# A four-layer graph network on one core: one run of activations ahead of the block norm, transfers issued in another order between stages, and maxima taken block by block

## What is computed

```python
# layer 0: two mean convolutions around a small MLP
h = relu(mean_in(x) @ Wl.T + bl + x @ Wr.T); h = relu(h @ M1.T + b1) @ M2.T + b2
out = mean_in(h) @ Wl2.T + bl2 + h @ Wr2.T
# layer 1: messages over the edges, then over the nodes; mlp = silu(batchnorm(. @ W + b))
msg = mlp(concat([x[src], edge_attr])); agg = mean of msg over dst
out = mlp(concat([x, agg]))
# layer 2: out = segment_sum((x @ W + b)[src] * att, dst)
# layer 3: three hops h = segment_sum(norm * h[src], dst), then h @ W + b
```

## Time and profile before

| | |
|---|---|
| median of 3 runs | 7751.79 us (7751.47 to 7754.62) |
| profiled execution, its own time | 7756.2 us |
| span of the profiled execution | 7754.3 us |
| busy PE, PEld, DVE, ACT, POOL | 5193.7, 4676.6, 2918.5, 1301.6, 3566.4 us |
| mean granted clock of PE | 0.823 of full speed |

### The profile page before, as it was taken

The page is one execution under the profiler, slowest core; times in us unless marked ns, Lnnn a source line. Parts: engine busy times, 40 slices in busy tenths (PEclk is TensorE's granted clock), DMA queues, the critical chain, the costliest instruction groups (busy, mean ns, idle before and its releaser), DMA issues.

```text
span 7754.3 us, 162987 instructions
## 1 busy us (share of the span) xinstructions
PE 5193.7 (67%) x62971; PEld 4676.6 (60%) x62971; DVE 2918.5 (38%) x5181; ACT 1301.6 (17%) x1613; POOL 3566.4 (46%) x3543
## 2 busy tenths in 40 slices
PE   5999989994444444444466336656656656999999
PEld 5999959993222222222255236655555656999999
DVE  6999931112111111111178434444444444111111
ACT  3777730000000000000066300000000000000000
POOL 2111100005777777777765177777777773000000
PEclk9999989996666666666699567777777778999999
DMA  4444408883333333333376113434434434898887
GB/s 118 186 180 184 185 34 263 275 277 101 94 94 95 95 95 95 95 95 95 92 232 194 36 34 104 110 94 110 111 94 111 111 94 139 274 293 281 275 273 242
DMA packets 559744, 1154.73 MB, mean 149 GB/s; under 512 B 155246, under 2 KB 367216, under 8 KB 546464
## 3 DMA queue, kind: packets, MB, share of 16 engines
q1 hardware_dynamic: 234784, 794.54, 32.1%
q10 hardware_dynamic: 215616, 239.17, 9.4%
q0 software_dynamic: 108896, 114.33, 7.3%
HBM read 898.83 MB, written 248.88 MB: 148 GB/s over the span
## 4 chain that ended last, share of the span: by engine, by line
POOL 36%; PE 26%; issue 16%; DVE 2%; ACT 2%; DMA 2%; DVEq 1%; POOLq 0%; ACTq 0%; SPq 0%; PEldq 0%
POOL gath L366 36%; PE banks L863 21%; PE banks L967 2%; DMA gath<-tab_l,idx 1%; DVE area L1898 1%; ACT gath L1387 1%; ACT banks L1384 1%; PE banks L544 1%; PE banks L556 1%; PE banks L1547 1%; PE banks L957 1%; DVEq L1910 0%; DMA gath<-counts 0%; ACT feat L1349 0%; PE banks L1542 0%
## 5 line engine op out<-in xcount | busy, mean ns | idle before, releaser
L366 POOL DMA_INDIRECT gath<-tab_l,idx x3328 | 3149.1, 946 | 2109.7 <-DMA idx<-src_idx 1096.3
L1556 PE MATMUL banks<-area,ones 128*128 128x448 f32 (+1 forms) x1040 | 674.0, 821 | 1205.1 <-DVE area L1840 1205.0
L967 PE MATMUL banks<-oneh,gath 128*64 128x128 f32 x3328 | 697.9, 404 | 891.9 <-DMA gath<-tab_l,idx 891.9
L1556 PEld LDWEIGHTS banks<-area,ones 128*128 128x128 f32 x1040 | 308.6, 312 | 1528.4 <-issue 1527.5
L967 PEld LDWEIGHTS banks<-oneh,gath 128*64 128x64 f32 x3328 | 658.5, 219 | 917.5 <-DMA gath<-tab_l,idx 917.5
L1840 DVE TENSOR_TENSOR area<-gath,banks 128x448 f32<-128x448 f32 (+1 forms) x256 | 138.9, 584 | 1660.1 <-DMA gath<-tab_l,idx 1653.6
L829 ACT CAST wide<-banks 128x784 uint16<-128x784 f32 x784 | 651.4, 858 | 221.9 <-PE banks L786 221.6
L798 PE MATMUL banks<-feat,wide 128*128 128x129 f16 x9604 | 670.7, 220 | 0.3 <-ACT wide L829 0.3
L798 PEld LDWEIGHTS banks<-feat,wide 128*128 128x128 fp8e4 x9604 | 606.3, 97 | 0.6 <-issue 0.5
L863 PE MATMUL banks<-wide,gath 128*128 128x128 f16 x9604 | 557.4, 220 | 20.4 <-DMA gath<-counts 20.4
L863 PEld LDWEIGHTS banks<-wide,gath 128*128 128x128 fp8e4 x9604 | 544.8, 98 | 22.2 <-issue 21.8
(11 more groups left out here) (257 smaller groups left out, 6542.4 us busy)
## 6 DMA issues: line engine op xcount, KB each, us to landing
gath<-counts SPq DMA_DIRECT2D x294, 784.0 KB, 4.5
oneh<-counts SPq DMA_DIRECT2D x294, 784.0 KB, 4.5
counts<-wide SPq DMA_DIRECT2D x98, 1568.0 KB, 5.2
gath<-counts ACTq DMA_DIRECT2D x98, 784.0 KB, 4.7
area<-counts ACTq DMA_DIRECT2D x98, 784.0 KB, 4.8
area<-edge_feat SPq DMA_DIRECT2D x128, 448.0 KB, 4.3
gath<-tab_l,idx POOLq DMA_INDIRECT x3328, 2.4
edge_h<-area ACTq DMA_DIRECT2D x128, 416.0 KB, 5.1
```

The source lines that it names most:

```text
L366: pool.indirect_dma_start(out=to[:, h, c, 0:H], out_offset=None, in_=table[:, :], in_offset=bass.IndirectOffsetOnAxis(ap=idx[:, slot, c:c ...
L967: last = T.matmul(window[h][0:H, :], near[:, h, c, :], oneh[:, h, c, :], start=(c == 0), stop=(c == C - 1))
L1556: ins = T.matmul(bank[n][:, 0:(hi - lo) * H], ones[:, :], src[:, lo:hi, :].rearrange("p c f -> p (c f)"), start=first and lo == 0, stop=la ...
```

## The change

1. **Setup.** ACT, no longer SP, issues the write of `fine_heads`, as its first instruction. DVE takes the maximum of each block as soon as that block is copied, `fine_dve` runs after the sixth block, and the last reduction is over 14 numbers. The bias fold of the residual is gone from here; `keep_root` adds the bias. The low parts of `x` are written by DVE in the first slot of the count matrix, behind its first one-hots, and PE waits for them at its first sums.
2. **MLP to dense pass.** `keep_root` takes the block's maximum too. High and low parts of `y` are written in seven pieces of 14 tiles, and PE waits piece by piece. SP begins to load the counts when the products of the count matrix are done.
3. **Dense to edge pass.** The first four lists are loaded ahead of the last table stores. ACT issues the load of `rdeg`, when the first edge group has been added; DVE waits for it only ahead of `z_means`.
4. **Norm stage.** ACT activates all 14 blocks in a row; then the turns have nine steps. PE has four pairs of banks and writes block b when block b - 4 has left them. `row_scale` moves to POOL, as step 9. The first four lists and the attention weights are issued behind the last store, ahead of the wait for it.

The core of the diff:

```diff
...
+x_peak = y_low = sem("block_maxima_then_y_low_pieces")
...
-d_norm = Turns("d_norm", 11, of=d_l1)
+d_norm = Turns("d_norm", 9, of=d_l1)
+s_silu, s_rows = p_conv2.onehot, p_conv2.summed
...
-def load_lists(sp, n_win, used, edge=False):
-    with sp.Fori(0, n_win) as w:
-        with sp.Fori(0, ITERS // 2) as j:
-            for v in range(2):
-                i = 2 * j + v
-                for h in range(2):
+def load_lists(sp, n_win, used, edge=False, ahead=False):
+    def lists(w, j):
+        for v in range(2):
+            i = 2 * j + v
+            for h in range(2):
+                if not (ahead and isinstance(j, int)):
...
-                    if edge:
-                        hold(sp, used, 2 * (w * ITERS + i) + h + 3)
-                        sp.dma_start(eft[:, h, :], group(edge_feat, 2 * i + h)).then_inc(s_ef[h], 16)
+                if edge:
+                    hold(sp, used, 2 * (w * ITERS + i) + h + 3)
+                    sp.dma_start(eft[:, h, :], group(edge_feat, 2 * i + h)).then_inc(s_ef[h], 16)
+    if ahead:
+        lists(0, 0)
+        with sp.Fori(1, ITERS // 2) as j:
+            lists(0, j)
+    else:
+        with sp.Fori(0, n_win) as w:
+            with sp.Fori(0, ITERS // 2) as j:
+                lists(w, j)
+def first_lists(sp):
+    for q in range(RING):
+        sp.dma_start(idx[:, q, :], group(src_idx, q)).then_inc(idx_in[q], 16)
...
-def store(sp, d, table):
+def store(sp, d, table, beside=lambda sp: None):
...
+    beside(sp)
...
+def rows_at(b):
+    u = b % 4
+    return banks[:, 2 * u:2 * u + 2, :].rearrange("p b n -> p (b n)")[:, 0:BN]
+def rows_and_products_of(u):
+    return rows_at(u).rearrange("p (t a f) -> p t a f", a=2, f=H)
...
-def scale_dve(dve, w, src, s):
-    V.tensor_reduce(top[:, w:w + 1], src, AX.XY, ALU.max, apply_absolute_value=True).then_inc(s, 1)
+def block_peak(src, b):
+    return V.tensor_reduce(peak[:, bass.ds(b, 1)], tiles(src, b), AX.XY, ALU.max, apply_absolute_value=True)
+def scale_dve(dve, w, s, peaks, blocks):
+    dve.wait_ge(peaks, blocks)
+    V.tensor_reduce(top[:, w:w + 1], peak[:, :], AX.X, ALU.max).then_inc(s, 1)
...
-def high_act(act, w, to, src, s):
+def high_act(act, w, to, src, s, step=NT):
...
-    S.activation(to, src, ACT.Identity, scale=scale[:, w, 0:1]).then_inc(s, 1)
-def low_dve(dve, w, to, src, high, s):
-    dve.wait_ge(s, 8)
-    V.scalar_tensor_tensor(to, src, scale[:, w, 0:1], high, ALU.mult, ALU.subtract).then_inc(s, 1)
+    for t in range(0, NT, step):
+        S.activation(to[:, t:t + step, :], src[:, t:t + step, :], ACT.Identity, scale=scale[:, w, 0:1]).then_inc(s, 1)
+def low_dve(dve, w, to, src, high, s, step=NT, made=None):
+    for n, t in enumerate(range(0, NT, step)):
+        dve.wait_ge(s, 8 + n)
+        V.scalar_tensor_tensor(to[:, t:t + step, :], src[:, t:t + step, :], scale[:, w, 0:1], high[:, t:t + step, :],
+                               ALU.mult, ALU.subtract).then_inc(s if made is None else made, 1)
...
+            if isinstance(j, int) and j == 0:
+                low_rows()
...
+            if isinstance(j, int) and j == 1:
+                pe.wait_ge(x_top, 9)
...
         for s in range(half * NT // 2, (half + 1) * NT // 2):
+            if k == 0 and isinstance(i, int) and i == t == 0 and s % ND_PAIR == 0:
+                pe.wait_ge(y_low, 2 * NB + s // ND_PAIR + 1)
...
-def back_to_rows(sp):
-    sp.dma_start(rdeg, degree_row.to_broadcast([H, NP])).then_inc(s_deg, 16)
+def back_to_rows(eng):
+    eng.dma_start(rdeg, degree_row.to_broadcast([H, NP])).then_inc(s_deg, 16)
...
-    load_lists(sp, 1, s_eh, edge=True)
+    load_lists(sp, 1, s_eh, edge=True, ahead=early)
...
-    store(sp, d_norm if early else d_l1, tab_l2)
-    sp.dma_start(att_s[:, :, :], att).then_inc(s_att, 16)
-    load_lists(sp, n_win, p_att.summed)
+    if early:
+        def lists_and_weights(sp):
+            first_lists(sp)
+            sp.dma_start(att_s[:, :, :], att).then_inc(s_att, 16)
+        store(sp, d_norm, tab_l2, beside=lists_and_weights)
+        load_lists(sp, 1, p_att.summed, ahead=True)
+    else:
+        store(sp, d_l1, tab_l2)
+        sp.dma_start(att_s[:, :, :], att).then_inc(s_att, 16)
+        load_lists(sp, n_win, p_att.summed)
...
-    sp.wait_ge(b_find, 1)
-    sp.dma_start(fine_heads, fine_f).then_inc(b_tab, 16)
...
             sp.wait_ge(b_st[u], 16 * TITERS)
+        sp.wait_ge(b_mm, GRP * NT)
+        sp.sem_inc(h_mm[0], 4)
...
         counts_in(sp, 0, each=store_last)
+        first_lists(sp)
...
         sp.sem_inc(s_table, 1)
-        sp.wait_ge(s_deg, 16)
-        back_to_rows(sp)
...
                     scaled(h, w * ITERS + i, 2 * (w * ITERS + i) + h)
+    if early:
+        def row_scale(b, h):
+            return pool.tensor_tensor(tiles(resid, b), nod[:, h, 1, :, :], over_features(ln[:, h, 1, :]), ALU.mult)
+        turns(pool, d_norm, [(9, row_scale)], written_out=True)
...
 def _(act):
+    act.wait_ge(b_find, 1)
+    act.dma_start(fine_heads, fine_f).then_inc(b_tab, 16)
...
-    high_act(act, 1, rows2[:, :, 0, :], y_lin, y_top)
+    high_act(act, 1, rows2[:, :, 0, :], y_lin, y_top, step=ND_PAIR)
...
+        if early:
+            act.wait_ge(s_deg, 16)
+            act.wait_ge(s_eh, RING + 1)
+            back_to_rows(act)
...
-            turns(act, d_norm, [(1, silu_in_place), (5, ln_square), (7, ln_std)])
+            for b in range(NB):
+                silu_in_place(b, b % 2).then_inc(s_silu, 1)
+            turns(act, d_norm, [(3, ln_square), (5, ln_std)], written_out=True)
...
-                d_norm.wait(pe, b // 2, b % 2, 2)
-                done(rows_and_product(b, b % 2), d_norm, b % 2)
+                pe.wait_ge(s_silu, b + 1)
+                if b >= 4:
+                    pe.wait_ge(d_norm.turn[b % 2], (b // 2 - 2) * d_norm.steps + 8)
+                rows_and_product(b, b % 2).then_inc(s_rows, 1)
...
-        pe.wait_ge(y_top, 10)
-        pe.sem_inc(h_mm[0], 4)
...
-    fine_dve(dve)
-    dve.wait_ge(b_res, 16)
-    fold_bias(R_BL2)
-    dve.wait_ge(x_ev, NB)
-    scale_dve(dve, 0, x_lin, x_top)
-    low_dve(dve, 0, rows1[:, :, H:2 * H], x_lin, rows1[:, :, 0:H], x_top)
-    build_dve(dve)
+    for g in range(NB):
+        dve.wait_ge(x_ev, g + 1)
+        block_peak(x_lin, g).then_inc(x_peak, 1)
+        if g == 5:
+            fine_dve(dve)
+    scale_dve(dve, 0, x_top, x_peak, NB)
+    build_dve(dve, lambda: low_dve(dve, 0, rows1[:, :, H:2 * H], x_lin, rows1[:, :, 0:H], x_top))
...
-        return V.tensor_scalar(tiles(y_root, b), hi_lo(h, 2)[:, :, 1, :], 1.0, None, ALU.mult)
+        kept_rows = V.tensor_tensor(tiles(y_root, b), hi_lo(h, 2)[:, :, 1, :], row_b(R_BL2), ALU.add)
+        block_peak(y_lin, b).then_inc(x_peak, 1)
+        return kept_rows
...
-    scale_dve(dve, 1, y_lin, y_top)
-    low_dve(dve, 1, rows2[:, :, 1, :], y_lin, rows2[:, :, 0, :], y_top)
+    scale_dve(dve, 1, y_top, x_peak, 2 * NB)
+    low_dve(dve, 1, rows2[:, :, 1, :], y_lin, rows2[:, :, 0, :], y_top, step=ND_PAIR, made=y_low)
...
-    dve.wait_ge(s_fold, 1)
-    V.tensor_tensor(resid[:, :, :], resid[:, :, :], y_root, ALU.add).then_inc(s_fold, 1)
+    dve.wait_ge(b_res, 16)
+    V.tensor_tensor(resid[:, :, :], resid[:, :, :], y_root, ALU.add).then_inc(s_fold, 2)
...
-    dve.wait_ge(y_top, 10)
+    dve.wait_ge(y_top, 7 + NT // ND_PAIR + 1)
...
+        if early:
+            dve.wait_ge(s_deg, 32)
...
-            return V.tensor_reduce(ln[:, h, 0, :], hi_lo(h, 0)[:, :, 0, :], AX.X, ALU.add)
+            dve.wait_ge(s_rows, b + 1)
+            return V.tensor_reduce(ln[:, h, 0, :], rows_and_products_of(b)[:, :, 0, :], AX.X, ALU.add)
...
-                                          hi_lo(h, 0)[:, :, 0, :], ALU.mult, ALU.add)
-        def row_scale(b, h):
-            return V.tensor_tensor(tiles(resid, b), nod[:, h, 1, :, :], over_features(ln[:, h, 1, :]), ALU.mult)
+                                          rows_and_products_of(b)[:, :, 0, :], ALU.mult, ALU.add)
...
-            return V.tensor_tensor(nod[:, h, 0, :, :], hi_lo(h, 0)[:, :, 1, :], over_features(ln[:, h, 1, :]),
-                                   ALU.mult)
+            return V.tensor_tensor(nod[:, h, 0, :, :], rows_and_products_of(b)[:, :, 1, :],
+                                   over_features(ln[:, h, 1, :]), ALU.mult)
...
-            turns(dve, d_norm, [(3, row_sum), (4, row_center), (6, ln_var), (8, ln_rstd), (9, row_scale),
-                                (10, product_scale), (11, product_bias)])
+            turns(dve, d_norm, [(1, row_sum), (2, row_center), (4, ln_var), (6, ln_rstd), (7, product_scale),
+                                (8, product_bias)], written_out=True)
+            for h in range(2):
+                dve.wait_ge(d_norm.turn[h], DITERS * d_norm.steps + 1)
```

(2 more changed lines are left out.)

5 lines of the change are left out of this document (2 added, 3 removed).

## The result

| | before | changed kernel |
|---|---|---|
| median | 7753.08 us (4 runs, 7751.47 to 7754.62) | 7633.98 us (4 runs, 7632.67 to 7642.59) |
| ratio | | 0.9849, 95% interval 0.9832 to 0.9866 |
| profiled execution, own time and span | 7756.2 and 7754.3 us | 7634.97 and 7633.2 us |

A forecast was written before the change was run, and what follows sets the result against it. POOL's gathers (36% of the span) and PE's stored-count products (21%) run at fixed pace, so only seams move: 28.0 + 20.6 + 20.3 + 56.1 = 125.0 us off 7751.8 gives 7626.8 us, range 7610 to 7656.

The forecast's parts named there:

- A: Seam from the start up to the count products: second one-hots at 94.3 instead of 122.32, gain 28.0 us.
- B: Seam between MLP and dense pass: PE starts at 1158.8 instead of 1179.42, gain 20.6 us.
- C: Seam between dense and edge pass: first gather at 1782.3 instead of 1802.60, gain 20.3 us.
- late raw ids: Bound in seam A: heads late by the whole 27 us, raw ids last; gain 15, or 13 us worse.
- A's delay in slot 0: Count pass: low parts delay DVE by 6.75 us, counted in full; up to 6.8 better if PE's slack swallows it.
- D: Norm stage up to the first attention gather: gather at 4353.1 instead of 4409.19, gain 56.1 us.
- D's half turn: Norm stage: DVE and POOL alternate at 4.05 us a block, thirteen of them ending at 4344.3.
- the two handovers: Norm stage: passing a block from DVE to POOL and back costs 0.27 and 0.15 us, both estimates.
- POOL's price at 1.05 delays the turn by 1.47: Norm stage: POOL's 448-wide row scale takes 1.05 us by width, 1.47 with handovers; bounds 0.62 and 1.94.
- The `rdeg` load: Rival in the edge pass: the load is not hidden and costs up to 20.5 us, giving 7647; chance 0.08.
- The seam that does not open: Rival: POOL's first edge gather still waits behind the old transfer, seam C gives nothing, 7647; chance 0.03.
- stay within 1 or 2 us: Sign: the lengths of the five passes between the seams should change by no more than 1 or 2 us.

The follow-up runs named there:

- Run 5: Changed kernel with the write of `fine_heads` back in SP's queue, behind the load of the residual: 7653.65 us.
- Run 7: Changed kernel with high and low parts between MLP and dense pass written as one instruction each again: 7631.12 us.
- run 11: Changed kernel with SP loading `rdeg` behind the table again and DVE waiting for it ahead of the edge pass, lists still early: 7649.38 us.
- run 12: Changed kernel with the first four edge lists issued behind the table again, the `rdeg` load staying on ACT: 7632.70 us.
- run 2: Changed kernel with the norm stage's row scale moved back from POOL to DVE, still as step 9: 7634.06 us.
- run 8: Run 7 with six semaphore counts added on DVE, which put its message-pass loop back to instruction 521: 7645.08 us.
- run 10: Changed kernel with POOL's row scale outside the turns, released by the inverse, and maxima of x over pairs of blocks (DVE's loop at 515): 7618.39 us.

## Why the prediction was right, and where its terms were off

- **The chains read backwards from each pass's first instruction** gave each seam within 1.0 us in A, B and C. Run 5 bears out A's split: with the heads late the seam loses 15.3, where the prediction had 13 for late raw ids. Run 7 bears out B's (10.1 against 5.52 + 6.75 less one piece of each), runs 11 and 12 C's. In C the first gather stands 3.8 us behind the end of the last row step, where I had 2.8 (1782.3 - 1779.52).
- **A's delay in slot 0.** I counted DVE's 6.75 us in full and put down 6.8 for the case that PE's slack swallows them. From the second one-hots on the pass took 890.9 against 889.6, and from the first ones 905.4 against 897.4; nothing was swallowed, and the count in full was right. Whether low parts ahead of the first one-hots would be as good was not tried, nor what the early request of the counts is worth by itself.
- **D's half turn was the mis-sized term**: 4.05 forecast, 3.62 measured, and 13 x 0.43 = 5.6 us of the 5.9 that the stage is shorter than forecast; what else differs (0.9 less up to the first root, 1.0 more behind the last) cancels. Three parts make the 0.43, less the 0.1 that I had taken off: DVE's 448-wide steps last 0.62 but start 0.54 apart when one does not wait for another, so that row sum to bias took 2.47 for 2.68; the two handovers to POOL and back took 0.19 and 0.03, where my estimates were 0.27 and 0.15; and POOL's step took 0.94, not 1.05. The Trainium skill, GPSIMD Engine Reference, section 4.1 Engine selection, has such work on GpSimd about twice as slow as on VectorE; the trace has 0.94 to 0.62, or 1.5 times, and the trace decides. My step "POOL's price at 1.05 delays the turn by 1.47" stood in the right place, since POOL was on the chain (measured, 1.16); but that the move was worth making is refuted by run 2.
- **The rivals.** The `rdeg` load was hidden: it is issued at 1754.45 and POOL goes on at 1.25 us a gather; the edge pass took 2098.6 for 2097.5. The seam that does not open was a true risk: run 11 is that case. No lower clock in the full passes: 1.00, 1.00, 0.99.
- **What I had not on the list**: that the passes between do not stay within 1 or 2 us. The message pass lost 5.7 us in a loop which the change does not touch. Runs 7, 8 and 10 show that six DVE instructions more or less ahead of it decide it, which one cannot see in the kernel's text. Without it the changed kernel would have been at about 7628 (7634.0 - 5.7, an estimate). The seams erred to the good by 4.4 us and the passes to the bad by 8.3, so that the forecast comes as near as 7 us to the median is in part luck. Which places are good is open: 495 and 515 are, 521 and 527 are not.

## What to carry to other kernels

Cost a change in the seams between paced passes one seam at a time, reading back from the first instruction of the next pass; the gains then added up here to within 8 us (129.4 against 121.1), of which the place of one loop took 5.7. A wait costs what stands behind it on its engine: one DVE wait for a load that nobody needed yet held back POOL's first gather by 17.4 us, through a count given behind it. And work moved to another engine paid here only once it had left the chain as well: with POOL's step waited for at once the move brought nothing, released at the moment its inputs were there it brought about 7 us.

## What the runs showed of the hardware that was not expected

- The same loop of four engines costs 2.57 or 2.62 us a group (329.1 or 334.8 over 128) by where DVE's part of it lies in the program; DVE shows it as a gap of 0.22 us or of 0.31 to 0.43 us, put down to "issue", once in each turn of its loop. That DVE fetches its program there is an explanation that was argued and not shown.
- A multiply of 448 elements took POOL 0.94 us, and one of 832 took 1.94: 2.1 ns an element in one and 2.3 in the other.
- A 448-wide step of DVE that waits for no other starts 0.54 us behind the one before it though it lasts 0.62, so a sum over mean durations is too high by a seventh.
- A gather instruction on POOL that starts while DVE runs an instruction with two inputs in SBUF ends 0.82 us behind the end of that one, in all 46 cases of this kind among the gathers of ids in the kernel before and all 44 in the changed one. In the kernel before, the first gather of edge ids (L674) took 7.14 us, from 83.81, beside the bias fold (83.45 to 90.13); the next three took 0.94 each beside the maximum, which has one input. In the count pass of both kernels such a gather takes 3.88 us when it starts with the first one-hots (3.4 us, two inputs) and 1.9 with the next ones (2.3 us). DVE, which reads the ids, never waited for them. With the bias fold gone from the setup, the first gathers of ids take 0.94 us each in the changed kernel.
